# A graph layer with a sort and a layer norm on one core: VectorE's part of a record moves to the head of its turn

## What is computed

```python
edge_feat = concat([h[dst], h[src], rel_pos, distance])      # E x 260
x = silu(edge_feat @ W1 + b1)
x = silu(x @ W2 + b2)
scores = (x @ W3 + b3)[:, 0]
alpha = segment_softmax(scores, dst)
msg = h[src] @ Wv * (alpha * node_weight[src])[:, None]
out = h + segment_sum(msg, dst)
result = layernorm(h + out)
```

## Time and profile before

| | us |
|---|---|
| median of 3 runs | 1025.85 |
| lowest, highest | 1018.76, 1027.38 |
| the profiled execution, its own time | 1024.02 |
| its span, first to last instruction | 1021.9 |
| POOL busy (issue gaps not counted) | 755.6 |
| DVE busy | 606.3 |
| PE busy | 584.4 |
| ACT busy | 515.4 |

### The profile page before, as it was taken

The page is one execution under the profiler, slowest core; times in us unless marked ns, Lnnn a source line. Parts: engine busy times, 40 slices in busy tenths (PEclk is TensorE's granted clock), DMA queues, the critical chain, the costliest instruction groups (busy, mean ns, idle before and its releaser), DMA issues.

```text
span 1021.9 us, 10972 instructions
## 1 busy us (share of the span) xinstructions
PE 584.4 (57%) x2391; PEld 342.2 (33%) x2391; DVE 606.3 (59%) x2374; ACT 515.4 (50%) x1217; POOL 755.6 (74%) x790
## 2 busy tenths in 40 slices
PE   0999988898954455677666666776667640000000
PEld 0544444444422233344344344444434440000000
DVE  7778787688653626897898788774434784000000
ACT  0465554655544666679798778884434332000000
POOL 6767767666777777777777777777777777777775
PEclk9968758775856778778877877787977755555555
DMA  6688889888984867686787867743222112111110
GB/s 202 204 268 294 299 254 320 272 278 284 277 320 161 286 243 282 216 313 238 254 298 240 314 207 281 246 158 86 71 82 70 58 52 70 45 45 46 46 46 27
DMA packets 77913, 198.00 MB, mean 194 GB/s; under 512 B 19007, under 2 KB 49409, under 8 KB 65304
## 3 DMA queue, kind: packets, MB, share of 16 engines
q1 hardware_dynamic: 49560, 134.37, 35.7%
q0 software_dynamic: 28288, 62.93, 21.6%
HBM read 106.64 MB, written 92.16 MB: 195 GB/s over the span
## 4 chain that ended last, share of the span: by engine, by line
DVE 25%; PE 19%; POOL 17%; issue 15%; DMA 3%; ACT 3%; POOLq 0%; SPq 0%; DVEq 0%; ACTq 0%
POOL out_rows L417 14%; DVE dst L884 5%; PE bank L621 5%; DVE m_q L958 4%; PE bank L608 4%; PE bank L615 4%; POOL hk L413 3%; DMA xin<-in_x 3%; PE bank L598 3%; PE bank L623 2%; DVE est L972 2%; ACT xin L469 2%; DVE hk L967 2%; DVE xin L899 1%; DVE drs L867 1%
## 5 line engine op out<-in xcount | busy, mean ns | idle before, releaser
L469 ACT ACTIVATE xin<-xin,drs 128x128 f32<-128x128 f32 x637 | 258.4, 485 | 74.0 <-DVE drs L869 74.0
L413 POOL DMA_INDIRECT region<-in_xw,snd_t x196 | 188.9, 964 | 77.9 <-issue 46.3
L417 POOL DMA_INDIRECT out_rows<-hk,sidx_t x196 | 191.8, 979 | 59.8 <-issue 58.8
L413 POOL DMA_INDIRECT region<-rec_d,id_t x196 | 186.7, 953 | 59.7 <-issue 59.7
L413 POOL DMA_INDIRECT hk<-in_x,kg_t x196 | 185.9, 949 | 59.8 <-issue 59.8
L573 PE MATMUL bank<-wsv,region 128*128 128x256 f32 x392 | 180.9, 553 | 27.8 <-DVE region L922 14.4
L884 DVE BATCH_NORM_STATS2 dst<-xin 128x6 f32<-128x256 f32 x392 | 137.1, 414 | 26.5 <-DMA xin<-in_x 26.1
L598 PE MATMUL bank<-region,m_q 128*128 128x128 f32 x392 | 74.5, 348 | 93.3 <-DVE m_q L958 93.3
L958 DVE TENSOR_SCALAR m_q<-bank,kcol,acol 128x128 f32<-128x128 f32 x196 | 74.0, 403 | 88.2 <-PE bank L637 84.2
L621 PE MATMUL bank<-hkT,w1a 128*128 128x512 f32 x98 | 67.6, 779 | 86.4 <-issue 66.9
L598 PEld LDWEIGHTS bank<-region,m_q 128*128 128x128 f32 x392 | 62.9, 244 | 105.5 <-DVE m_q L958 105.5
(11 more groups left out here) (179 smaller groups left out, 870.1 us busy)
## 6 DMA issues: line engine op xcount, KB each, us to landing
xin<-in_x SPq DMA_DIRECT2D x49, 1024.0 KB, 7.2
out_rows<-xin SPq DMA_DIRECT2D x49, 1024.0 KB, 4.6
rec_d<-region SPq DMA_DIRECT2D x49, 512.0 KB, 6.7
region<-in_xw,snd_t POOLq DMA_INDIRECT x196, 5.8
hk<-in_x,kg_t POOLq DMA_INDIRECT x196, 4.0
region<-rec_d,id_t POOLq DMA_INDIRECT x196, 3.1
out_rows<-hk,sidx_t POOLq DMA_INDIRECT x196, 2.2
ef_d<-hk SPq DMA_DIRECT2D x9, 196.0 KB, 3.4
```

The source lines that it names most:

```text
L413: pool.indirect_dma_start(out=to, out_offset=None, in_=frm, in_offset=bass.IndirectOffsetOnAxis(ap=index, axis=0)).then_inc(done, 16)
L417: pool.indirect_dma_start(out=out, out_offset=bass.IndirectOffsetOnAxis(ap=index, axis=0), in_=frm, in_offset=None, bounds_check=N - 1, oo ...
L469: ins = nc.scalar.activation(xin[:, j % X_RING, n, :], xin[:, j % X_RING, n, :], ACT.Identity, bias=drs[:, j % 2, 1, n:n + 1], scale=drs[: ...
```

## The change

The block of seven lines in DVE's loop of the first phase that takes its part of record j = i-1 moves from behind the sort to the head of the turn. Nothing is added or taken away. The order within a turn was: normalise, statistics, sort (with the chain between its steps), record, rest of the chain. It becomes: record, normalise, statistics, sort (with the chain), rest of the chain.

```diff
             for i in range(B0):
                 steps = SORT_PLAN[i] if i < len(SORT_PLAN) else 0
+                if i >= 1:
+                    j = i - 1
+                    wait_ring(dve, rec_out, j - REC_RING, 16)
+                    wait(dve, "AM_ready", 2 * j + 2)
+                    w = hs[:, j % HS_RING, 2:4, H:H + 1].to_broadcast((P, 2, H))
+                    vec.tensor_copy(rec[:, j % REC_RING, 2:4, 0:H], pair(j, 2)[:, :, 0:H])
+                    ins = vec.tensor_tensor(rec[:, j % REC_RING, 2:4, H:RW], pair(j, 2)[:, :, H:RW], w, ALU.mult)
+                    ins.then_inc(S["rec23"], 1)
                 dense_norm(i)
                 dense_stats(i)
                 for n in range(steps):
@@
                     next(network, None)
                     more(2)
                 more(6)
-                if i >= 1:
-                    j = i - 1
-                    wait_ring(dve, rec_out, j - REC_RING, 16)
-                    wait(dve, "AM_ready", 2 * j + 2)
-                    w = hs[:, j % HS_RING, 2:4, H:H + 1].to_broadcast((P, 2, H))
-                    vec.tensor_copy(rec[:, j % REC_RING, 2:4, 0:H], pair(j, 2)[:, :, 0:H])
-                    ins = vec.tensor_tensor(rec[:, j % REC_RING, 2:4, H:RW], pair(j, 2)[:, :, H:RW], w, ALU.mult)
-                    ins.then_inc(S["rec23"], 1)
                 more(99)
```

## The result

| | before | after |
|---|---|---|
| median of 6 runs each | 1022.83 | 1079.72 |
| lowest, highest | 1018.76, 1027.38 | 1075.69, 1084.73 |
| the profiled execution, its own time | 1024.02 | 1081.61 |
| its span | 1021.9 | 1079.5 |
| first gather of `hk` on POOL | 267.6 | 326.61 |

The kernel became slower: the ratio after to before is 1.0552, interval [1.0524, 1.0581]; by the profiled executions it is +57.6 us. The forecast was 1089 us with a range of 1055 to 1100.

The account below looks back on a forecast made before the run. POOL was taken as the bound, held in the first phase by records through a 16.1 us load loop. The last sender group's +69.3 us, less 4.5, gave +65 on 1024.0: 1089 us, range 1055 to 1100.

Parts of the forecast that it names:

- The load's wait: DVE's 12 waits for block loads, 25.4 us, vanish; by itself this would win POOL at most 15.9 us.
- The new loop: Statistics and chain of u, ACT's normalisations and copy, products and record u+2, statistics of u+3: 19.8 us against 16.1.
- the sum: First phase: start, eleven cycles of 19.8 us, flips, turns 37 to 42; last sender group +69.3, less 4.5 for full-clock cycles.
- The clock: PE's products behind the wait for ACT run at half clock in 9 of 11 cycles; two at full clock give back 4.5 us.
- The flips: In turns 27, 30, 33 and 36 PE waits for record and sort: 1.0, 0.7, 1.9 and 1.4, together 5 us.
- Start and end: Record 3 finished at 52.9; from block 37's statistics 24.4 us, then 32.1 us, to record 42.
- The record write at the end: Record 48 finished at about 368.6, its write of some 7 us needed by 377: tight, a few us upwards.
- POOL's waits: POOL's waits for DVE's part of a record grow to 4 to 5 us a cycle, 70 to 85 us in sum.
- The one in which only the load's wait goes: ACT's edge closes no loop, so the kernel gains 15.9 us, 1008 us; 4 in 100.
- The rival at full clock throughout: Same loop at 17.5 us: 192.7 for eleven cycles, 12 less in turns 37 to 42, 4 at start; 1057 us, 15 in 100.

Follow-up runs that it names:

- the head in block turns: The kernel before with the record moved to the head only in turns 1, 4, ... 46, before a block's statistics: 1320.12 us, ratio 1.0233 (before 1284.02).
- ACT's delay: The kernel after with ACT normalising and SP storing each block one turn later: 1299.62 us, ratio 1.0123; on a second chip 1281.10 us, 1.0143.
- The kernel with no loss: The kernel before with the record moved to the head in all turns except 1, 4, ... 46: 1267.48 us, ratio 1.0025 (before 1265.33).

## Why the prediction was right

**The load's wait goes.** Said: the 25.4 us vanish. Measured: 2.4, and 3.2 in the whole span.

**The new loop and its length.** The mechanism was the one named, link by link, and the runs with the head in block turns and with ACT's delay bear it out. Size: said 19.76 us at half clock and 17.5 at full clock. The cycle shown above is 19.42 us, with the first product pair still at full clock (0.70 us where the sum had 1.06 for the first pair of its row and 1.22 for the others); at half clock throughout it would be about what was said. The next one at full clock is 17.36. Chain to copied: 6.36 to 6.40, said 6.40.

**The clock.** Said: half clock for the first products behind the gap in 9 of 11 cycles. Windows of 2 us of the kernel after: PE, PEld, DVE, ACT, POOL busy; PEclk; DMA share; GB/s.

```profile
142.00:144.00 2.00, 0.39 (x2) 0.30 (x2) 1.16 (x4) 2.00 (x7) 1.39 (x3) 1.00 0.69 200
144.00:146.00 2.00, 2.00 (x7) 0.93 (x6) 0.00 (x0) 0.87 (x4) 1.54 (x2) 0.61 0.99 365
...
156.00:158.00 2.00, 2.00 (x6) 0.62 (x4) 1.97 (x8) 1.70 (x5) 0.00 (x0) 0.50 0.30 91
158.00:160.00 2.00, 2.00 (x10) 1.12 (x10) 1.59 (x8) 2.00 (x7) 0.00 (x0) 0.98 0.00 0
...
164.00:166.00 2.00, 2.00 (x9) 1.01 (x9) 0.00 (x0) 0.90 (x3) 1.70 (x2) 1.00 1.04 434
```

PE stands still from 140.5 to 143.6; the granted clock stays at 1.00 until past 144 and falls to 0.50 (1.2 GHz) only when PE works again, so here the products pay for a gap that is already over. It then stays there until about 158 though PE is busy all the time. In the next cycle the gap is 2.3 us (160.4 to 162.7), and the clock survives it. After the long gap of the cycle behind that (PE waits 7.1 us, until 180.75) the fall comes inside the gap, while PE does nothing, and the products again find the clock low:

```profile
174.00:176.00 2.00, 0.00 (x0) 0.00 (x0) 1.97 (x9) 1.66 (x5) 0.93 (x1) 0.79 0.41 105
176.00:180.00 4.00, 0.00 (x0) 0.00 (x0) 3.72 (x14) 4.00 (x12) 0.94 (x1) 0.50 0.40 131
```

By the durations of the product pairs in front of a block turn (1.22 us or 0.70), one of the eleven cycles had them all at full clock (the one of 17.36 us) and three in part (18.2, 18.8 and 19.4 us); the other seven had them at half clock throughout. The four together are 5.3 us below four cycles of 19.76, against the 4.5 us that the prediction took off for two whole ones; that the two amounts are so near is in part luck. Where the clock is low all the time, PE's wait for the copy is short: 0.48 us at 104 and at 124, since the work at half clock nearly fills the cycle, as the sum had it (18.6 us of work).

**The flips: the step that failed.** Said: 5 us in sum in turns 27, 30, 33 and 36, from PE waiting for record and sort before the flip. The kernel after, timelines of PE and ACT in turn 33:

```profile
237.48 0.69 PE L543 MATMUL bank<-ident,region 128*128 128x128 f32 x2 [5.09 <-DVEq L720]
...
238.13 0.59 ACT L478 ACTIVATE region<-bank 128x512 f32<-128x512 f32 x1
...
238.81 1.17 PE L573 MATMUL bank<-wsv,region 128*128 128x256 f32 x2
```

PE does wait for DVE's hand-over, 5.09 us, but the flip ends at 238.17, before the copy does at 238.72, and the products could not have started any earlier. Both waits lie side by side. The four cycles with a flip are 18.2, 19.9, 19.9 and 19.9 us; the four without one and with half clock throughout are 19.5, 19.5, 19.9 and 20.4, mean 19.8. That leaves some 0.1 us for a flip, not 1.2. The eleven cycles took 212.7 us where the sum had 217.4 + 5 - 4.5 = 217.9. This is 5.2 of the 7.4 us by which the forecast was too high.

**Start and end.** Record 3 was finished at 52.39, said 52.9. From block 37 to 40 it took 24.2 us (said 24.4), from there to block 43 32.1 us (said 32.1). The last sender group is 321.62 against 327.4 (331.9 with the 4.5 taken off); the 5.8 us are the cycles' 5.2 and the start's 0.5. The remaining 1.5 us are from the second phase, which the sum had as unchanged.

**The record write at the end.** It was said to be tight. DVE's last records were earlier by the same amount as all else, and POOL's first sorted gather shows only its issue gap of 0.30. The tightness cost nothing.

**POOL's waits.** Said 70 to 85 us. Measured 39.3 + 36.9 = 76.2. But half of them are for ACT's part of a record (line 486), not DVE's; the prediction named only line 922. ACT's part stands behind the same wait for the chain.

**The rivals.** The one in which only the load's wait goes would have been 1008 us. It needs the loop to be absent; the earlier load on its own, in the kernel before, came near it: 1009.49. The rival at full clock throughout is added up wrongly: from +69.3, its 24.7, 12 and 4 us leave +28.6, that is 1053 and not 1057 us, just under the stated range. It did not come, with seven of eleven cycles at half clock. The move gives the load a turn more as well, but binds DVE, ACT and PE together by it.

## What to carry to other kernels

Before an instruction is moved ahead of another on one engine, write down for each of the two what waits for it on the others, and follow that round until it comes back to the engine: count over how many turns the ring closes and what its links sum to. Here a move that took 25 us of visible waits away closed a ring of 19.4 us where the cycle had been 16.0, since the ring through ACT's in-order queue now closed in one cycle and not in two. If a wait for a load is what bothers, issue the load earlier; on the chip where those waits were seen that alone gave 13 us, with no other order touched, and on a slower one nothing.

## What the runs showed of the hardware

- TensorE's granted clock can fall after a gap as well as in it: behind the gap of 3.1 us that ended at 143.6 it fell with PE working again (0.61 in 144 to 146), and in the gap that ended at 180.75 it fell while PE stood (0.79 in 174 to 176, 0.50 behind it). A gap of 2.3 us, 160.4 to 162.7, left it at 1.00, but in 198 to 200, round a gap of 1.6 us, it fell (0.76, then 0.50). So the length of the gap alone does not tell.
- It can stay low under work: PE ran from 144.4 to 158 us without a pause at 1.2 GHz, and from 92 to 112 us it was busy for 19.52 of 20 us with a granted clock of 0.50 throughout.
- The same kernel took 1022.64 us on one chip and 1265 to 1284 us on three others. The kernel with no loss, the one with the head in all but block turns, shows it on one of them (page, groups: busy, mean ns of one | idle before, releaser):

```profile
L967 DVE TENSOR_SCALAR m_q<-bank,kcol,acol 128x128 f32<-128x128 f32 x196 | 74.0, 403 | 281.4 <-remote 193.3
```

This line's own time is what the kernel after had on the first chip (74.0 us), but its idle time is 281.4 us where that had 92.4, and the profile puts 193.3 of it to nothing on the core. A change to the order of the first phase kept its sign there (+44 for +57), but the gain of the earlier load was gone. What is slow there, the chip or something beside it, stays open.
